# A gated cross-attention and expert layer: the same instructions in another order

## The reference

```python
# block 1: local attention with 16 heads of 16, windows of 64 tokens,
# each window sees itself (causal) and the window before it
q = layernorm(x) @ W_q.T + b_q ; k = ctx @ W_k.T + b_k ; v = ctx @ W_v.T + b_v
sim = where(full_mask, (q * scale) . k, min)          # per head, 64 x 128 a window
x = x + tanh(g_xattn) * (softmax(sim) @ v @ W_o.T + b_o)
# block 2: top-1 router over 16 experts, capacity 160 tokens an expert, ranks in token order
probs = softmax(layernorm(x) @ gate_w.T) ; top1 = argmax ; rank = cumsum(one_hot(top1)) - 1
h = gelu(dispatch @ w1[e]) ; y = h @ w2[e]            # per expert, 256 -> 1024 -> 256
x = x + tanh(g_ffn) * probs[top1] * y                 # only where rank < capacity
```

## Time and profile before

| | us |
|---|---|
| median of 3 runs | 324.27 (322.58 to 327.51) |
| the profiled execution | 323.56 |
| its span, from the first to the last instruction | 321.8 |
| TensorE busy (matmuls) | 300.3, 93% |
| VectorE, ScalarE, GpSimd busy | 195.4, 177.1, 165.5 |
| granted TensorE clock | 0.995 of full speed |

### The profile page before, as it was taken

How to read it: one execution, slowest core, us unless ns; L and a number is a source line. 1 busy time by engine, 2 the same in 40 slices (tenths; PEclk the granted TensorE clock), 3 DMA queues, 4 the chain that set the end, 5 groups by cost and what they waited for, 6 DMA issues and landing times.

```text
span 321.8 us, 8449 instructions
## 1 busy us (share of the span) xinstructions
PE 300.3 (93%) x2759; PEld 245.3 (76%) x2760; DVE 195.4 (61%) x950; ACT 177.1 (55%) x666; POOL 165.5 (51%) x201
## 2 busy tenths in 40 slices
PE   7869879999999999999899999999999999999994
PEld 3438746887758866777788788888988989898974
DVE  2888898898999879899974331423325161515133
ACT  3479999999999999999755111111110202111110
POOL 6379647789769974989857112131313121121222
PEclk9997999999999999999999999999999999999999
DMA  7921299017512290230324689598979797997900
GB/s 217 280 95 25 81 378 298 5 26 239 189 67 91 58 305 3 94 86 9 92 98 182 173 234 353 171 364 255 365 226 368 216 367 245 310 305 246 373 20 13
DMA packets 48471, 60.55 MB, mean 188 GB/s; under 512 B 14712, under 2 KB 41360, under 8 KB 46384
## 3 DMA queue, kind: packets, MB, share of 16 engines
q1 hardware_dynamic: 44976, 53.20, 51.6%
q0 software_dynamic: 2560, 6.25, 5.3%
q10 hardware_dynamic: 896, 0.61, 0.6%
HBM read 44.60 MB, written 14.19 MB: 183 GB/s over the span
## 4 chain that ended last, share of the span: by engine, by line
PE 50%; ACT 26%; DVE 9%; issue 6%; DMA 4%; SPq 3%; POOL 1%; POOLq 0%; DVEq 0%; ACTq 0%
ACT probs L714 18%; PE bank L1765 18%; PE bank L1790 14%; PE bank L1815 4%; PE bank L1426 3%; ACT probsT L727 3%; DVE probs L960 3%; DMA w<-in_L_ffn_w_dram 2%; ACT q_par L688 2%; SPq L331 2%; PE bank L1437 2%; PE bank L1539 2%; PE bank L1479 1%; DMA x_all<-in_x_dram 1%; PE bank L1501 1%
## 5 line engine op out<-in xcount | busy, mean ns | idle before, releaser
L714 ACT ACTIVATE probs<-probs,low 128x128 f32<-128x128 f32 x256 | 99.3, 404 | 2.2 <-DVE low L960 2.2
L535 POOL TENSOR_TENSOR probs<-probs,r_total 128x512 f32<-128x512 f32 x64 | 66.4, 1047 | 18.4 <-DVE r_total L969 18.0
L1765 PEld LDWEIGHTS bank<-xdT,w 128*128 128x128 f32 x480 | 66.5, 190 | 2.8 <-issue 2.2
L1765 PE MATMUL bank<-xdT,w 128*128 128x160 f32 x480 | 68.0, 300 | 0.6 <-issue 0.4
L960 DVE CUSTOM_DVE_ANT_0 probs<-bank,mask_now 128x128 f32<-128x128 f32 x256 | 57.2, 283 | 7.6 <-PE bank L1467 7.2
L714 ACT ACTIVATION_READ_ACCUMULATOR probs<-probs,low 128x1 f32 x256 | 52.4, 205 | 0.0
L884 ACT ACTIVATE w_raw<-bank 128x480 f32<-128x480 f32 (+1 forms) x24 | 12.6, 526 | 61.4 <-PE bank L1765 57.6
L639 POOL DMA_INDIRECT out_dram<-base,place x16 | 14.0, 875 | 59.0 <-DVE base L1325 38.2
L648 POOL DMA_INDIRECT out_dram<-base,place x16 | 15.7, 980 | 53.8 <-DVE place L1318 43.6
L884 ACT ACTIVATE x_all<-bank 128x480 f32<-128x480 f32 (+1 forms) x24 | 12.6, 527 | 53.2 <-PE bank L1765 53.2
L1335 DVE SCALAR_TENSOR_TENSOR base<-bank,base 128x256 f32<-128x256 f32 x15 | 7.2, 482 | 51.7 <-PE bank L1790 51.6
(11 more groups left out here) (148 smaller groups left out, 495.4 us busy)
## 6 DMA issues: line engine op xcount, KB each, us to landing
w<-in_L_ffn_w_dram SPq DMA_DIRECT2D x32, 1024.0 KB, 7.1
expert_queue<-empty_row SPq DMA_DIRECT2D x1, 5140.0 KB, 17.7
q_blocks<-expert_queue SPq DMA_DIRECT2D x62, 40.0 KB, 3.0
base<-expert_queue SPq DMA_DIRECT2D x16, 129.0 KB, 4.6
ctx_rows<-in_ctx_dram SPq DMA_DIRECT2D x4, 512.0 KB, 9.7
out_dram<-rows SPq DMA_DIRECT2D x4, 512.0 KB, 6.3
x_all<-in_x_dram SPq DMA_DIRECT2D x3, 512.0 KB, 7.7
v_shift<-v SPq DMA_DIRECT2D x12, 128.0 KB, 2.3
```

What stands on the lines that cost most here:

```text
L535: pool.tensor_tensor(probs[:, i % NP_], probs[:, i % NP_], r_total[:, i % NP_].unsqueeze(2).to_broadcast([P, PAIRS, 2 * WINDOW]), ALU.mult ...
L714: last = act.activation(probs[:, i % NP_, j], probs[:, i % NP_, j], ACT.Exp, scale=-1.0, bias=low[:, i % NP_, j:j + 1], accum_out=total[:, ...
L1765: last = pe.matmul(ps_hidden[m][:, c * CAP:(c + 1) * CAP], w1_sb[i % 2][:, k, f * P:(f + 1) * P], xdT[i % 2][:, k], start=(k == 0), stop=( ...
```

## The change

The calls of the batch loop and of the last batch stand in another order, in the lists of VectorE, TensorE, ScalarE and also GpSimd. The set of calls, their operands, buffers and semaphore values are the same; waits that stood ahead of a call moved with it. SyncE's list and the experts' phase are as before, but for `turn_queued_xd`, whose definition and call moved up in VectorE's list. Below are the parts that matter; the remaining differences are moves of the same kind by one to three places.

```diff
@@ gpsimd, batch loop
             for b in range(LAST):
+                x1_norm(b - 1, 0)
                 norm(b, 1)
-                scatter(b - 2, 2)
                 norm(b, 2)
-                scatter(b - 2, 3)
...
                 x1_rstd_of(b - 1, 1)
+                scatter(b - 2, 2)
                 norm(b, 6)
...
+                norm(b, 10)
+                scatter(b - 2, 3)
+                norm(b, 11)
+                norm(b, 12)
                 base_of(b + 1)
...
                 scatter(b - 1, 0)
+                scatter(b - 1, 1)
+                x1_rstd_of(b, 0)
                 norm(b, 15)
-                scatter(b - 1, 1)
                 norm(b + 1, 0)
-                x1_rstd_of(b, 0)
-
+                mask_of(b + 2)
@@ gpsimd, last batch
             norm(LAST, 15)
+            x1_norm(LAST - 1, 3)
             x1_rstd_of(LAST, 0)
             scatter(LAST - 1, 0)
+            scatter(LAST - 1, 1)
+            scatter(LAST - 1, 2)
             x1_rstd_of(LAST, 1)
-            scatter(LAST - 1, 1)
             x1_rstd_of(LAST, 2)
-            scatter(LAST - 1, 2)
             scatter(LAST - 1, 3)
@@ scalar, batch loop
                 exp(b, 0)
+                take_k(b, 1, ps_wide)
                 exp(b, 1)
-                take_k(b, 1, ps_wide)
                 take_q(b, 1, ps_misc)
...
                 exp(b, 5)
+                exp(b, 6)
+                take_xnT(b + 1, 0, ps_misc)
+                exp(b, 7)
                 take_probsT(b, 1)
-                exp(b, 6)
-                exp(b, 7)
-                take_xnT(b + 1, 0, ps_misc)
-                take_probsT(b, 3)
                 take_x1nT(b - 1, 0)
                 exp(b, 8)
+                take_probsT(b, 3)
                 take_ctxT(b + 1, 0, ps_wide)
+                take_xnT(b + 1, 1, ps_misc)
                 exp(b, 9)
                 take_ctxT(b + 1, 1, ps_wide)
                 take_probsT(b, 5)
-                take_xnT(b + 1, 1, ps_misc)
+                take_x1nT_or_gate(b - 1, ps_misc)
                 exp(b, 10)
-                take_x1nT_or_gate(b - 1, ps_misc)
                 exp(b, 11)
@@ scalar, last batch
             take_k(LAST, 1, ps_wide)
-            exp(LAST, 2)
             take_q(LAST, 1, ps_misc)
             take_probsT(LAST - 1, 13)
+            exp(LAST, 2)
@@ vector, batch loop
                 r_total_of(b, 8)
-                take_probsT(b, 4)
+                x_stats(b + 3)
+                x_norm(b + 2)
                 low_of(b, 12)
                 low_of(b, 13)
+                take_att(b, 0)
                 r_total_of(b, 9)
-                take_att(b, 0)
-                x_stats(b + 3)
-                x_norm(b + 2)
...
+                take_probsT(b, 10)
+                low_of(b + 1, 0)
                 r_total_of(b, 13)
-                mask_set_of(b + 1)
-                low_of(b + 1, 0)
                 r_total_of(b, 14)
+                rank_of(b - 1)
                 low_of(b + 1, 1)
-                take_probsT(b, 10)
-                rank_of(b - 1)
+                r_total_of(b, 15)
                 x1_of(b, 0)
                 x1_stats(b, 0)
-                r_total_of(b, 15)
+                r_total_of(b + 1, 0)
@@ vector, last batch
-            x1_of(LAST, 0)
-            x1_stats(LAST, 0)
-            take_att(LAST, 2)
             rank_of(LAST - 1, step=3)
             weights_of(LAST - 1, step=6)
+            x1_stats(LAST, 0)
...
             x1_stats(LAST, 2)
+            turn_queued_xd()
             mark_slots(LAST - 1, range(2, T))
             choose(LAST)
@@ tensor, batch loop
+                pe.wait_ge(xnT_taken, value(b + 1, 2, 2))
+                x1nT_or_gate(b - 1, ps_misc)
+                probsT_of(b, 6)
                 scores(b, 3)
                 pe.wait_ge(ctxT_taken, value(b + 1, 2, 2))
                 attend(b, 0)
-                pe.wait_ge(xnT_taken, value(b + 1, 2, 2))
-                x1nT_or_gate(b - 1, ps_misc)
-                probsT_of(b, 6)
-                probsT_of(b, 7)
```

More of the change, by code:

```diff
@@ L597, in _ @@
                 scatter(b - 1, 0)
+                scatter(b - 1, 1)
+                x1_rstd_of(b, 0)
                 norm(b, 15)
-                scatter(b - 1, 1)
                 norm(b + 1, 0)
-                x1_rstd_of(b, 0)
+                mask_of(b + 2)
+            scatter(LAST - 2, 2)
             norm(LAST, 1)
-            scatter(LAST - 2, 2)
             norm(LAST, 2)
+            norm(LAST, 3)
             scatter(LAST - 2, 3)
-            norm(LAST, 3)
             norm(LAST, 4)
@@ L610, in _ @@
             norm(LAST, 5)
+            norm(LAST, 6)
+            norm(LAST, 7)
             x1_norm(LAST - 1, 1)
             x1_rstd_of(LAST - 1, 1)
-            norm(LAST, 6)
-            norm(LAST, 7)
             norm(LAST, 8)
@@ L1179, in _ @@
                 r_total_of(b, 2)
+                low_of(b, 5)
                 take_probsT(b - 1, 14)
-                low_of(b, 5)
                 low_of(b, 6)
+                low_of(b, 7)
+                take_v(b, 0, ps_misc)
+                take_att(b - 1, 3)
                 r_total_of(b, 3)
-                low_of(b, 7)
-                take_att(b - 1, 3)
-                take_v(b, 0, ps_misc)
+                take_probsT(b, 0)
                 r_total_of(b, 4)
-                take_probsT(b, 0)
+                low_of(b, 8)
                 r_total_of(b, 5)
-                low_of(b, 8)
                 r_total_of(b, 6)
@@ L1238, in _ @@
             low_of(LAST, 4)
+            r_total_of(LAST, 2)
             low_of(LAST, 5)
-            r_total_of(LAST, 3)
             low_of(LAST, 6)
             low_of(LAST, 7)
+            r_total_of(LAST, 3)
+            take_att(LAST - 1, 3)
+            r_total_of(LAST, 4)
+            take_v(LAST, 0, ps_misc)
             take_probsT(LAST, 0)
-            take_v(LAST, 0, ps_misc)
-            r_total_of(LAST, 4)
-            take_att(LAST - 1, 3)
+            r_total_of(LAST, 5)
             low_of(LAST, 8)
             low_of(LAST, 9)
+            r_total_of(LAST, 6)
             take_probsT(LAST, 2)
-            r_total_of(LAST, 5)
             low_of(LAST, 10)
-            r_total_of(LAST, 6)
+            x1_of(LAST - 1, 1)
             r_total_of(LAST, 7)
-            x1_of(LAST - 1, 1)
             x1_stats(LAST - 1, 1)
             r_total_of(LAST, 8)
-            low_of(LAST, 11)
             take_probsT(LAST, 4)
             take_att(LAST, 0)
-            low_of(LAST, 12)
+            low_of(LAST, 11)
+            take_v(LAST, 1, ps_misc)
             r_total_of(LAST, 9)
             take_probsT(LAST, 6)
+            low_of(LAST, 12)
             r_total_of(LAST, 10)
             low_of(LAST, 13)
-            take_v(LAST, 1, ps_misc)
             low_of(LAST, 14)
@@ L1370, in pair @@
                     take_y(e + 1, i + 1)
-            turn_queued_xd()
             take_first_xd()
@@ L1636, in _ @@
                 v_of(b, 1, ps_misc)
+                probsT_of(b, 3)
                 if first:
@@ L1717, in _ @@
             x1nT_of(LAST - 1, 1)
+            scores(LAST, 3)
             probsT_of(LAST, 7)
             probsT_of(LAST, 8)
+            pe.wait_ge(v_taken, value(LAST, 2, 2))
+            route(LAST - 1)
+            probsT_of(LAST, 9)
             pe.wait_ge(x1nT_taken, value(LAST - 1, 2, 2))
             attend(LAST, 1)
-            probsT_of(LAST, 9)
-            pe.wait_ge(v_taken, value(LAST, 2, 2))
-            route(LAST - 1)
             probsT_of(LAST, 10)
+            probsT_of(LAST, 11)
             pe.wait_ge(att_taken, value(LAST, CHUNKS, 2))
             project(LAST, 0)
-            probsT_of(LAST, 11)
+            attend(LAST, 2)
             probsT_of(LAST, 12)
-            attend(LAST, 2)
             probsT_of(LAST, 13)
```

113 lines of the change are left out of this document (54 added, 59 removed).

## The result

The changed kernel takes 326.80 us (median of 6 runs, 325.27 to 327.37) beside 323.54 for the kernel before on the same chip. The ratio is 1.0096, with a 95% interval from 1.0073 to 1.0119: 3.1 us or 1% slower, small but clear of no change. The prediction was 321.7 with a range to 325.5; it had the wrong sign and missed its range.

The account below looks back on a forecast made before the run. ScalarE, the fullest engine, was taken to bound the batches, with the end following the last scatter. 323.56 - 2.2 (loop) - 0.3 (last batch) + 0.6 (router's tail) = 321.7 us, range 319.0 to 325.5.

Parts of the forecast that it names:

- The loop's gain of 2.2: Three loop batches: most of ScalarE's 2.77 us idle goes, 0.8 of it counted as gain; bounds 0 and 2.8.
- The waits named: ScalarE's idle places in the batches: 0.50 for transposed context, 0.54 and 0.61 for q products, 0.32 for a score tile.
- no cost is added: Whole change: no instruction is added or removed, so no cost by itself; only who stands behind whom changes.
- The sentence on base_of: GpSimd in the loop: moved mask_of and base_of are hidden in its 8.7, 6.3 and 6.9 us idle.
- The loops with "1.1 to spare": ScalarE's waits for k and q: round trips of 2.5 and 3.0 us against 3.56 and 4.13 of ScalarE work.
- The third rival: Ports collide: x_norm in batches 0 and 1 lets two GpSimd norms through, 2.1 us each time, 325.9; chance 0.07.
- The last batch: +0.3: take_q(3, 1) before exp(3, 2) fills ScalarE's 0.32 wait at 130.01; gain 0.3 of 0.31 us.
- The router's tail: a loss of 0.6: GpSimd at the router's end: three scatters ahead of both rstd's delay the last rstd; loss 0.6 us, bounds 0 and 1.1.
- stays there: Router's end: first scatter remains at 163.60, its 2.22 us of idle using up the later statistics on VectorE.
- The tail decides: Rival: router's end consumes the loop's gain, scatters start no earlier and rstd is 1.1 late; 324.7 us; chance 0.15.
- The gaps only move: Rival in the batches: waits saved at q return at low or probsT, loop keeps 0.9, 323.0 us; chance 0.25.
- exp waiting for low in every batch: Sign in ScalarE's batches that the forecast would be wrong; no size given.

Follow-up runs that it names:

- mended: Changed kernel with rank_of ahead of r_total 13 and 14, base_of behind norm(b, 6), and the last batch's lists as before; 323.36 us, ratio 0.9995.
- marks_alone: mask_back with r_total_of(b, 10) and (b, 11) moved behind choose(b - 1) on VectorE; 322.62 us, ratio 0.9959.
- loop_only: Changed kernel's loop with all four lists of the last batch as in the kernel before; 325.04 us, ratio 1.0045.
- mask_back: mended with mask_set_of(b + 1) back directly ahead of low_of(b + 1, 0) on VectorE; 322.63 us, ratio 0.9958.
- rank_first: Changed kernel with rank_of(b - 1) ahead of r_total 13 and 14 in VectorE's loop; 324.97 us, ratio 1.0049.
- rank_base: rank_first with base_of(b + 1) back behind norm(b, 6) on GpSimd; 324.25 us, ratio 1.0019.
- last_only: Kernel before's loop with the changed lists of the last batch; 324.33 us, ratio 1.0023.
- tail_pool: Changed kernel with GpSimd's scatters and rstd's at the router's end taking turns as before; 325.62 us, ratio 1.0074.
- tail_norm: Changed kernel with x1_stats(LAST, 0) directly behind x1_of(LAST, 0) and x1_norm(LAST - 1, 3) back behind norm(LAST, 9); 324.87 us, ratio 1.0039.
- before_r14: Kernel before with r_total_of(b, 14) moved directly ahead of rank_of(b - 1) in VectorE's loop; 324.22 us, ratio 1.0028.

## Why the prediction was wrong

*The loop's gain of 2.2 (bounds 0 and 2.8).* The waits named did go from batches 0 and 1, which are 1.2 and 0.5 shorter than before, 1.7 in all, and mended and marks_alone keep that (33.41 and 33.42, both 35.60). The step that failed is the sentence that no cost is added since no instruction is, and with it the lower bound of 0. The same instructions took longer: `rank_of` 2 x 1.16, and in batch 2 `choose` 1.1 and `mask_set` and `weights_of` together 1.1. The sentence on base_of ("moved on GpSimd", hidden in its idle time) failed in the same way: GpSimd had the time, but `weights_of` stood beside it. loop_only measured a loss of 1.5 in the place of a gain of 2.2. With `rank_of`, `base_of` and `mask_set` put back out of each other's way and the rest of the loop kept (mask_back), it is a gain of 1.4 (0.7 to 2.0). That is what the term was worth.

*The loops with "1.1 to spare".* For q I added 0.17, 0.75, 1.88 and 0.2 as if `x1_of` could start once exp 15 was over. In the list `rank_of` and a low stand ahead of it. At 2.35 for `rank_of`, `x1_of` started at 90.92 (the sum puts it at 87.7) and q came 1.12 late; at 1.19 in rank_first q is still 0.46 late, and only in rank_base and mended, with `base_of` moved too, is that wait gone. The product for k, with the same margin, came 0.21 late. The margin was 1.1, the stretch 1.16 for each `rank_of`, and I had written that `rank_of` comes earlier without asking what r_total 13 and 14, now directly ahead of it, start on GpSimd.

*The third rival (0.07).* Its mechanism was right and its place wrong. x_norm beside norms took 1.55 and 2.16 (before 1.35 and 1.73), so 0.2 and 0.4 more and not 2.1 each, and nothing of it reached ScalarE, as the text said. That its 325.9 comes nearest to what was measured is luck. The Trainium skill, "SBUF — State Buffer", section "Who interferes with whom", speaks of more than the tensor_scalar that I applied it to: a VectorE operation with two SBUF inputs contends with GpSimd's reads too, one with at most one SBUF input outside the two-port modes doesn't, and a reduction never does. The traces agree. In after, `seen`, `slot_f` and `onehot` were stretched, to 0.52, 1.00 and 1.71, while rank's reduction was 0.22 each time, the 256 of low 0.26 to 0.29 and the 30 copies of probsT from PSUM 0.65 to 0.69, with norms beside them or not. Had I gone down VectorE's list with that sentence, `rank_of` behind two r_totals would have stood out.

*The last batch: +0.3.* It was worth nothing. In last_only, with the loop of before, the 0.32 ahead of exp(3,2) is gone, but ScalarE idles 0.22 for q instead (at 130.07), and exp(3,0) to exp(3,4) takes 9.99 for 9.94. In the changed kernel VectorE's delay from the loop comes on top: 1.75 ahead of exp(3,1) and 0.55 for q.

*The router's tail: a loss of 0.6 (bounds 0 and 1.1).* The part that was worked out, the scatters' order, was right: 0.56 (tail_pool), and 0.53 in last_only (from the first scatter to exp_last_logits 5.94 for 5.41). The whole was too small: 0.7 by the ratio (last_only, 0.0 to 1.5), 0.8 from rank_base to mended, and by the traces 1.1 and 1.0 from exp(3,0) to the last scatter, the upper bound. In the changed kernel, where VectorE arrives late, the two edits of tail_norm gave back 1.8 by the ratios and 1.4 at the last scatter, 0.2 of it by exp(3,0); why they give as much as last_only's whole loss with the scatters' order still in isn't settled. What was wrong is that the first scatter "stays there". In last_only the last copy of transposed probabilities was 1.2 earlier than before and that scatter still 0.9 later (164.50), bound by rstd(3,0), which waited for statistics behind `rank_of` (1.75 for 1.19, beside norm 15) and `weights_of`. I had named this and let the 2.22 of idle time absorb it.

*Rivals.* "The tail decides", slower at 324.7, had the sign right, with a cause that carries a quarter to a third of the loss. "The gaps only move" isn't refuted: the waits are gone from batches 0 and 1, but in the third batch even mask_back, the version with the fewest collisions, has 0.50 for q and 0.26 for probsT. What I named as a sign of error, exp waiting for low in every batch, is what the trace shows in batches 2 and 3. The end follows the scatters, 3.1 later, but not exactly one for one: in after TensorE waits 1.26 for a load of w at 214.09, and from the last scatter to the end the fourteen profiles need 144.4 to 146.0.

The account, in us against before, by the ratios: changed +3.1; rank_of -1.5; base_of -1.0 (0.2 by the trace); the last batch's lists -0.8; mask_set -1.2; left -1.4. Each step has some 1.0 of uncertainty, so only those of rank_of and mask_set are clear of it by time. The steps also depend on their order: from changed to loop_only the last batch's lists give 1.6, and from there to mended rank_of and base_of together 1.6. What stays open is the rest to the 2.2: in mask_back ScalarE still idles 0.50 for q(3,0) at 115.73, 0.26 at 121.70 for probsT and 0.64 at 130.18 for low, and I haven't tried to remove these.

## What to carry to other kernels

An order of work is also an order of neighbours: for each call that is moved, ask what it releases on the other engine and which operations of one's own then run beside that. Short VectorE operations on SBUF (two inputs, or a wide bf16 tensor_scalar) belong where GpSimd is idle, ahead of what releases its work and not behind it; those that read PSUM and reductions can fill the time beside it. Compare the busy time of an engine whose work is unchanged: 2 us more of it is the first sign, before any wait.

## What the hardware showed

A VectorE operation that is held can stay held over two GpSimd operations that follow each other without a gap: 2.44 us for one of 0.41, in mended and in rank_base. Not each time, though: in after `seen` got out between norm 13 and 14, and `mask_set` between norm 12 and `base_of`, 0.3 after the norm's end (122.20 and 121.92); what decides it isn't settled. The price follows what GpSimd runs, and not the size of the operation: 1.00 for `slot_f` with four elements a partition.

TensorE's granted clock fell in batch 0 in ten of the fourteen profiled executions, and cost differently. The stretches from 22 to 30 us of mended, then of mask_back, which differ only in what comes after 46 us:

```profile
22.00:26.00 4.00, 2.24 (x37) 2.02 (x38) 3.96 (x20) 4.00 (x17) 2.79 (x3) 1.00 0.01 2
26.00:30.00 4.00, 2.46 (x41) 1.99 (x41) 4.00 (x31) 4.00 (x22) 3.69 (x5) 1.00 0.00 0
```

```profile
22.00:26.00 4.00, 2.19 (x33) 1.97 (x34) 3.48 (x13) 4.00 (x18) 2.79 (x2) 0.68 0.02 6
26.00:30.00 4.00, 4.00 (x11) 3.17 (x12) 3.88 (x34) 3.75 (x20) 3.43 (x5) 0.50 0.00 0
```

At 0.50, the lower of its two levels (1.2 for 2.4 GHz), TensorE is busy all of 26 to 30; from 18 to 22, before the clock fell, it was busy for 3.1 of 4.0, as in mended. It is late from there, and exp(0,12) comes 1.4 later (45.65 for 44.22). Batch 0 is 34.78 long for 33.41 in mended; in loop_only, with 0.50 in the same place, it is 34.79. In after the clock was 0.64 from 26 to 30, and its batch 0 was as long as with the full clock, 33.41. In the old order the batch took 34.6 both at 0.67 (before) and at 1.00 (before_r14); no profile has it at 0.50. So in the new order one execution can be 1.4 longer than another for this alone, as much as the gain that was sought; the medians and intervals, not the two profiles, decide here.
